# SyncE issues the loop's loads behind the first four pairs, and the constants, the last values and the DRAM fill behind the loop

## What is computed

```
x = x + xattn(layernorm(x), ctx, ctx, mask, Wq, bq, Wk, bk, Wv, bv, Wo, bo)   # 16 heads of 8, 257 keys
x = x + attn(layernorm(x), w_q, w_k, w_v, w_o)                                # rotary, 16 heads on 4 key heads
x = x + ffn(layernorm(x), Wg, W1, W2)                                         # 8 experts, chosen per expert by top_k
```

```
energy = einsum('bhqd,bhkd->bhqk', Q, K) * scale
energy = where(mask == 0, -1e9, energy)
out = einsum('bhqk,bhkd->bhqd', softmax(energy), V)
```

## Time and profile before

| | us |
|---|---|
| median of 3 runs (775.78 to 777.36) | 776.03 |
| span of the profiled execution | 779.7 |
| PE busy in that span | 682.9 |
| DVE busy | 621.1 |
| ACT busy | 470.1 |
| POOL busy | 417.4 |

### The profile page before, as it was taken

How to read it: one execution, slowest core, us unless ns; L and a number is a source line. 1 busy time by engine, 2 the same in 40 slices (tenths; PEclk the granted TensorE clock), 3 DMA queues, 4 the chain that set the end, 5 groups by cost and what they waited for, 6 DMA issues and landing times.

```text
span 779.7 us, 29152 instructions
## 1 busy us (share of the span) xinstructions
PE 682.9 (88%) x9915; PEld 534.1 (68%) x9915; DVE 621.1 (80%) x1462; ACT 470.1 (60%) x1499; POOL 417.4 (54%) x439
## 2 busy tenths in 40 slices
PE   4732999999999999999999975599999949999995
PEld 2421767777777777777777754478777737888894
DVE  6413899999999999999999966769888956779584
ACT  2731767777777777777777743435555533545552
POOL 4650385465455456354453417757777747506376
PEclk9985999999999999999999998979999957999998
DMA  7497444444444444444443003000000020002531
GB/s 169 98 160 183 84 95 87 89 87 96 88 89 96 84 92 95 85 97 85 83 81 67 1 3 108 2 3 4 4 0 0 4 68 2 1 1 83 192 116 42
DMA packets 186526, 55.05 MB, mean 71 GB/s; under 512 B 146708, under 2 KB 184856, under 8 KB 186466
## 3 DMA queue, kind: packets, MB, share of 16 engines
q1 hardware_dynamic: 183344, 49.88, 30.4%
q0 software_dynamic: 1824, 3.96, 1.5%
q10 hardware_dynamic: 1298, 0.40, 0.2%
HBM read 44.51 MB, written 8.83 MB: 68 GB/s over the span
## 4 chain that ended last, share of the span: by engine, by line
PE 59%; SPq 14%; issue 8%; ACT 6%; DVE 6%; POOL 4%; ACTq 1%; DMA 1%; DVEq 0%; POOLq 0%
PE bank L484 25%; PE energy L484 20%; PE bank L487 14%; SPq L515 9%; ACT PR L632 5%; DVE STAT L1531 2%; SPq L521 2%; SPq L538 1%; POOL SX L923 1%; POOL TQ L915 1%; DMA MK<-in_mask_BxSxS_ik 1%; PE energy L487 1%; ACTq L632 1%; SPq L503 1%; SPq L506 0%
## 5 line engine op out<-in xcount | busy, mean ns | idle before, releaser
L632 ACT ACTIVATE PR<-energy,STAT 128x256 f32<-128x256 f32 x512 | 234.8, 484 | 116.8 <-DVE STAT L1531 116.8
L1531 DVE TENSOR_REDUCE STAT<-energy 128x512 f32 (+1 forms) x256 | 164.3, 685 | 27.1 <-PE energy L484 26.9
L487 PE MATMUL bank<-ident,PR 128*128 128x128 f32 x1024 | 151.9, 282 | 31.6 <-DVE PT L1548 28.0
L1548 DVE COPY PT<-bank 128x512 f32<-128x512 f32 x256 | 161.8, 671 | 0.8 <-PE bank L487 0.8
L487 PEld LDWEIGHTS bank<-ident,PR 128*128 128x128 f32 x1024 | 109.3, 141 | 62.6 <-issue 50.9
L820 POOL TENSOR_TENSOR QB<-QT,headmask 128x512 f32<-128x512 f32 x32 | 33.3, 1041 | 191.2 <-DMA MK<-in_mask_BxSxS_ik 121.9
L632 ACT ACTIVATION_READ_ACCUMULATOR PR<-energy,STAT (+1 forms) x512 | 110.4, 216 | 0.0
L827 POOL TENSOR_SCALAR MZ<-MK 128x512 bf16<-128x512 int32 x64 | 94.3, 1490 | 7.2 <-DMA MK<-in_mask_BxSxS_ik 7.2
L484 PEld LDWEIGHTS bank<-wv_s,CT 128*128 128x128 f32 x512 | 67.2, 192 | 31.3 <-issue 31.3
L1504 DVE STREAM_TRANSPOSE CT<-CX 128x512 f32<-128x512 f32 x64 | 44.9, 701 | 32.3 <-DMA CX<-in_ctx 29.3
L484 PE MATMUL bank<-PT,VT 128*32 128x128 f32 x2048 | 70.0, 278 | 0.3 <-DVE PT L1548 0.3
(11 more groups left out here) (265 smaller groups left out, 1295.6 us busy)
## 6 DMA issues: line engine op xcount, KB each, us to landing
CX<-in_ctx SPq DMA_DIRECT2D x512, 32.0 KB, 2.5
MK<-in_mask_BxSxS_ik SPq DMA_DIRECT2D x128, 128.0 KB
rows_in<-fill SPq DMA_DIRECT2D x1, 3483.0 KB, 21.2
X<-in_x SPq DMA_DIRECT2D x4, 512.0 KB, 7.3
VLT<-v_last SPq DMA_DIRECT2D x4, 512.0 KB, 9.8
PAY<-rows_in SPq DMA_DIRECT2D x2, 903.0 KB, 8.2
PAY<-X SPq DMA_DIRECT2D x1, 1280.0 KB, 6.8
w_s<-in_L_ffn_W SPq DMA_DIRECT2D x1, 1024.0 KB, 5.6
```

Of the source, the lines that this page charges most:

```text
L487: return nc.tensor.transpose(o, i, ident[0:n, 0:n])
L632: nc.scalar.activation(PR[:, b, g, :], EB[:, g, e * KEYS:(e + 1) * KEYS], ACT.Exp, bias=STAT[:, bass.ds(t, 1), b, 1, g:g + 1].rearrange("p ...
L1531: V.tensor_reduce(STAT[:, bass.ds(t, 1), b:b + 2, 1, g:g + 1].rearrange("p a b g -> p (a b g)"), EB[:, g, :].rearrange("p (e k) -> p e k", ...
L1548: V.tensor_copy(PT[:, k % 2, e, 2 * half:2 * half + 2, :].rearrange("p g k -> p (g k)"), psum[1 if e else 7]).then_inc(ev_t, 1)
```

## The change

On SP the loop over the pairs 4 to 63 is put directly behind the pairs 0 to 3. Behind the loop follow the constants, ML, VLT, then W1 and W2 with their wait for `ev_o`, and last the fill of the DRAM table. On POOL the wait for the constants, the work on them and MLB are moved behind the loop over the tiles, ahead of the last three `keep_own`; KLB stays ahead of the loop, now without the constants before it. No instruction is added or removed.

```
+            with sp.Fori(1, NP // 4) as i:
+                for k in range(4):
+                    load_pair(i * 4 + k, k, False)
             for dst, src in small_s:
                 sp.dma_start(dst[:, :], src).then_inc(ld_s, 16)
...
+            sp.wait_ge(ev_o, NP)
+            sp.dma_start(w1_s[:, :, :], W1.rearrange("e c f -> c e f")).then_inc(ld_ffn, 16)
+            sp.dma_start(w2_s[:, :, :, :], W2.rearrange("e (j f) c -> f e j c", f=P)).then_inc(ld_ffn, 16)
             sp.wait_ge(fill_ok, 2)
             sp.dma_start(rows_in.rearrange("(k p) c -> p k c", p=P),
...
-            with sp.Fori(1, NP // 4) as i:
-                for k in range(4):
-                    load_pair(i * 4 + k, k, False)
-            sp.wait_ge(ev_o, NP)
-            sp.dma_start(w1_s[:, :, :], W1.rearrange("e c f -> c e f")).then_inc(ld_ffn, 16)
-            sp.dma_start(w2_s[:, :, :, :], W2.rearrange("e (j f) c -> f e j c", f=P)).then_inc(ld_ffn, 16)
...
             tile(1, 1, False)
 
+            pool.wait_ge(klt_ok, 1)
+            nc.gpsimd.tensor_tensor(
+                KLB[:, :, :], KLT[:, :].rearrange("p (n a) -> p n a", a=1).broadcast_to([P, NB, 16]),
...
+            with pool.Fori(2, NT // 2) as i:
+                for k in range(2):
+                    tile(i, k, False)
             pool.wait_ge(ld_s, N_S)
...
-            pool.wait_ge(klt_ok, 1)
-            nc.gpsimd.tensor_tensor(
-                KLB[:, :, :], KLT[:, :].rearrange("p (n a) -> p n a", a=1).broadcast_to([P, NB, 16]),
...
             pool.wait_ge(ld_ml, 16)
             nc.gpsimd.tensor_scalar(MLB[:, :], ML[:, :], 0.0, BIG, ALU.is_equal, ALU.mult).then_inc(mlb_ok, 1)
-            with pool.Fori(2, NT // 2) as i:
-                for k in range(2):
-                    tile(i, k, False)
             for t in range(NT - 3, NT):
                 keep_own(t, t % 2)
```

More of the change, by code:

```diff
@@ L873, in _ @@
             tile(1, 1, False)
+            pool.wait_ge(klt_ok, 1)
+            nc.gpsimd.tensor_tensor(
+                KLB[:, :, :], KLT[:, :].rearrange("p (n a) -> p n a", a=1).broadcast_to([P, NB, 16]),
+                head16[:, :].rearrange("p (a h) -> p a h", a=1).broadcast_to([P, NB, 16]), ALU.mult)\
+                .then_inc(klb_ok, 1)
+            with pool.Fori(2, NT // 2) as i:
+                for k in range(2):
+                    tile(i, k, False)
             pool.wait_ge(ld_s, N_S)
@@ L889, in _ @@
                 nc.gpsimd.tensor_copy(sw_vg[:, g, g * HD:(g + 1) * HD], sw_v[:, g * HD:(g + 1) * HD]).then_inc(wqk_ok, 1)
-            pool.wait_ge(klt_ok, 1)
-            nc.gpsimd.tensor_tensor(
-                KLB[:, :, :], KLT[:, :].rearrange("p (n a) -> p n a", a=1).broadcast_to([P, NB, 16]),
-                head16[:, :].rearrange("p (a h) -> p a h", a=1).broadcast_to([P, NB, 16]), ALU.mult)\
-                .then_inc(klb_ok, 1)
             pool.wait_ge(ld_ml, 16)
             nc.gpsimd.tensor_scalar(MLB[:, :], ML[:, :], 0.0, BIG, ALU.is_equal, ALU.mult).then_inc(mlb_ok, 1)
-            with pool.Fori(2, NT // 2) as i:
-                for k in range(2):
-                    tile(i, k, False)
             for t in range(NT - 3, NT):
```

## The result

The changed kernel takes 750.78 us (median of 4 runs, 749.82 to 752.30) where the kernel before took 776.69 beside it (4 runs, 775.78 to 780.25): a ratio of 0.9665, with a 95% interval from 0.9640 to 0.9691. Two later comparisons, on two chips and with more runs, gave 0.9630 (0.9602 to 0.9658) and 0.9633 (0.9607 to 0.9659). So the change is faster by 26 to 28 us, as forecast in kind; the measured 750.8 us lies 0.8 us above the upper end of the range, 744.8 to 750.0, and 4.3 us above the forecast.

A forecast was written before the change was run, and what follows sets the result against it. The late loads of pair 4, behind SP's constants, ML, VLT and fill, were taken as the bound at 47 to 73 us, PE beyond. 27.1 + 2.4 = 29.5 us off 776.03 gave 746.5 us, range 744.8 to 750.0.

The forecast's parts named there:

- The loads of pair 4: Ramp, 47 to 73 us: DVE's wait for CX goes, pair 3 starts on PE at 51.32, not 78.40; 27.1 us gained.
- The term of 27.1 us: Gain from pair 4's earlier loads, read at PE's start of pair 3: 51.32 instead of 78.40.
- The pairs 3 to 8: Five steps on PE take 30.25 us, not 32.70, as SP's lead suffices; 2.4 us gained, ends 2.45 and 0.
- the 2.45 us: Pairs 3 to 8: excess of 32.70 us over 30.25 at full pace, put down to the loads.
- The rival of the ramp: Pairs 3 to 8 keep their loss, lead too small or masks slow: 748.7 to 749.0 us; chance 0.14.
- The pairs 8 to 63 and the tail: Loop at 341.43 us, set by PE, and the moved constants, MLB, VLT, W1, W2 and fill behind it: 0 change.
- The two terms of cover at the tail, for the constants and for VLT: Behind the loop on POOL: 4.9 us of cover left for the constants, 28 us for VLT; cost 0.
- The tail's rival: Behind the loop, VLT's transfer beside written-out code causes issue gaps of 2.38 us: 748.9 to 751.3 us; chance 0.10.
- I carry the gain over in us, as it is one wait and no share of the rest: 776.03 - 29.5: Whole kernel: the profiled execution's gain of 29.5 us taken unscaled from the median of 776.03, giving 746.5 us.
- the gain of 29.5: Sum of 27.1 us for pair 4's loads and 2.4 us for pairs 3 to 8; profiled execution 779.7 to 750.2.
- What would have shown it wrong: Profile signs: DVE idle for CX or PE for MZ in ten pairs, tail gaps or waits, SP never waiting in the loop.

The follow-up runs named there:

- the kernel with MZ later: Changed kernel, with POOL making MZ of pair 0 behind all its normalisations of the queries, not in their middle: 748.45 us, ratio 0.9616.
- the last kernel: The kernel with MZ later, with four small first tensors issued from ACT's queue instead of SP's ahead of pair 0: 748.06 us, ratio 0.9580.
- the second more profile of the kernel before: The kernel before, run again unchanged for one more profiled execution: 780.31 us, span 778.4.
- the two of its faster offspring: Changed kernel with POOL's MZ of pair 0 later, 748.45 us; that plus four small tensors moved from SP's to ACT's queue, 748.06 us.
- the three of the experiments between: Kernel before, fill alone moved behind W1 and W2: 767.77 us; changed kernel, fill ahead of the loop: 759.25; changed kernel, constants and ML ahead: 757.99.

## Why the prediction was off, point by point

**The loads of pair 4: right.** Pair 4's transpose at 44.97 and 44.29 (forecast 44.3), pair 3 on PE 6.04 us behind pair 2 (forecast 6.05). The term of 27.1 us was read from the profile on record, where pair 3 comes 33.1 us behind pair 2; in the other three it is 30.7 to 32.3, so the term is 24.7 to 27.1.

**The pairs 3 to 8: right in time, its lead misjudged.** 30.25 us in all three profiles of the changed kernel, as forecast. Pair 4's lead is 58.09 - 32.27 = 25.8 us, not 23.7, and it does not fall to 22.0 at pair 8 but is 82.29 - 56.24 = 26.1 there: SP needs 6.0 us a pair, not the 6.47 taken from the ramp. The measure was the wrong one besides. I took 20.1 us from a context's issue to PE's step as just enough, but in the kernel with MZ later pair 8 has 22.8 us and its step is still long, and in the last kernel it has 22.7 and is not. It is the second mask of a tile that tells (9.3 us and 11.4). The prediction put the 2.45 us to CX alone; in that trace POOL's MZ holds pair 6 up too, by 0.72 us on PE:

```profile
97.68 0.39 PE L484 MATMUL energy<-MZ,SEL_Q 32*128 32x512 bf16 x4 [0.72 <-POOL MZ L827]
```

The rival of the ramp fell here, since the lead was ample. Its rule from the Trainium skill (DMA: Bandwidth & Descriptors, Rules for kernel authors), that a broadcast of four copies runs on at most four engines, was not tested; that POOL's waits in the ramp are for MK fits it, but would also follow from the masks' place behind the contexts, and no view shows engines apart.

**The pairs 8 to 63 and the tail: forecast as unchanged, a little better.** In the means of the profiles the loop is 342.1 before and 340.7 after, the tail 327.7 and 326.0. The 1.4 us of the loop are the ramp's loss once more, all of it ahead of pair 13. The start is 0.9 us later, which nothing here explains. The two terms of cover at the tail, for the constants and for VLT, held: POOL does not wait for them, and from pair 63 to W1L, POOL's first step for the expert weights, it takes 44.5 to 45.6 us before and 45.4 to 45.8 after. The tail's rival fell: while SP issues VLT, from 399 to 407 us, and it is under way, PE works 11.97 us of 12 at a DMA share of 0.99, where a gap of 2.38 us was feared. Window of the changed kernel, columns as in the earlier trace rows:

```profile
400.00:412.00 12.00, 11.97 (x156) 9.10 (x148) 11.60 (x20) 9.63 (x36) 8.56 (x20) 1.00 0.99 148
```

The rule of the Trainium skill behind that rival (DMA: Bandwidth & Descriptors, Queues, rings and completion order), that each DMA engine goes round the queues it has work for, may hold; a fetch slowed by it cost nothing that this row shows.

**The step that failed: "I carry the gain over in us, as it is one wait and no share of the rest: 776.03 - 29.5".** Two numbers of different executions met in it. For the execution that was profiled the gain was read rightly: its span was to go from 779.7 to 750.2 us, and the changed kernel's spans are 747.9 to 750.1. But the median of 776.03 belongs to other, shorter executions, and between medians the gain is smaller: 25.9 (its interval allows 24 to 28), 28.0 and 28.4 us in the three comparisons. On the chip of the result that makes 3.6 of the 4.3 us by which the forecast was missed; the other 0.7 is the baseline, 776.69 and not 776.03.

The profiles show where the difference sits. The stretch that the change empties, pair 2 to pair 13, grows with the length of the execution (table above), by some 0.6 us for each us of span. An estimate from that line, with a median's span taken as its time less 1.9: 94.4, 95.4 and 96.9 us at 776.69, 778.42 and 780.90, less the changed kernel's 67.4 a gain of 27.0, 28.0 and 29.5, beside the 25.9, 28.0 and 28.4 measured. Four points carry it, and none is as short as the medians of 776, so it is an estimate and no more. That the gain of 29.5 comes near the 29.7 by which the mean of the profiles falls from pair 2 to pair 13 is partly luck: the prediction's sum ends at pair 8, where the profile on record had an uncommonly long stall and a short loss behind it. Why the stretch varies is open.

The warning stood on the page. The profiled execution was 3.7 us above the median by its span; with the 1.9 us outside the span, which I didn't know then, 5.6 us. I called the gain "no share of the rest". By the line above, some 3.4 of these 5.6 us were in the gain, and 776.03 - (29.5 - 3.4) = 749.9. If all of it had been, the answer would have been 776.03 - (29.5 - 5.6) = 752.1; the two readings, 746.5 and 752.1, should have been the range.

**What would have shown it wrong** did not come: no DVE wait for CX, no PE wait for MZ, no waits of POOL for constants. The sign came out as forecast, but the range was too narrow: the prediction took the scatter of three runs (0.25 us below and 1.3 above) for that of the kernel, whose runs spread from 775.1 to 784.9 over four comparisons.

## What to carry to other kernels

Here a big transfer ahead of a loop's loads cost them far more than its issue took: a fill issued in 0.47 us drew the loads behind it out to 14.95. So look in the first loads of a loop for a long issue (17.69 us for what takes 3.85), and put big transfers that nobody awaits behind the loop. Compare the lead of the loads with the one that just sufficed in the trace, and take it from the last load that a step waits for, since a consumer that starts earlier must be fed earlier too. And before a gain is read from one profiled execution, set that execution's time against the other runs: part of an excess may sit in the very wait that the change removes.

## What the runs showed of the hardware that was not expected

The same kernel before took medians of 776.7, 778.4, 778.5 and 780.9 us in four comparisons, three of them on chips known to differ, and its single runs spread over almost 10 us.

Part of the spread lies at the start of self attention, where PE is little busy (3.76 us of the first 10 behind W1L in the changed kernel's first profile) and its granted clock falls to 0.50, the lower of its two levels. When the clock rises again differs. Windows behind W1L (columns as in the earlier trace rows), 5 us each, of the changed kernel's first profile and of the second more profile of the kernel before:

```profile
478.30:483.30 5.00, 4.50 (x50) 3.79 (x48) 0.77 (x3) 0.76 (x2) 1.76 (x2) 0.50 0.01 3
483.30:488.30 5.00, 4.69 (x149) 3.68 (x149) 4.04 (x9) 2.04 (x5) 2.73 (x4) 0.86 0.02 3
```

```profile
505.86:510.86 5.00, 4.50 (x50) 3.79 (x48) 0.78 (x3) 0.76 (x2) 1.76 (x2) 0.50 0.02 3
510.86:515.86 5.00, 5.00 (x140) 3.94 (x139) 3.23 (x7) 1.68 (x5) 2.04 (x3) 0.50 0.00 0
515.86:520.86 5.00, 5.00 (x110) 3.83 (x79) 3.45 (x8) 1.85 (x5) 3.71 (x5) 0.50 0.01 3
```

The first has its clock up some 17 us behind the start of W1L; the other, after the same work in the first 15 us, is still at 0.50 at 25 us, with PE busy without a pause for the last 10. By POOL's first step of a tile there (QKR), a tile takes 3.8 to 4.9 us while the clock is low, and the first ones after take 2.9 to 3.6. The three profiles of the changed kernel and the two of its faster offspring all have one such slow tile; the four of the kernel before and the three of the experiments between have two to five. In the five the clock had fallen 2.6 to 3.0 us behind the start of W1L and rose at 16.2 to 16.6, in the seven others it fell at 4.7 to 5.4 and rose at 18.7 to 29.2 (read from the profile in slices of 1 us). The 1.7 us by which the tail is shorter all lie behind W1L, and the smaller number of slow tiles is the likely reason, not a shown one. Whether this goes with the change or with chance is open; no experiment here touched it.
